# Weighing a gathered tile in four half-size operations instead of two

## The chip, the cores and the metric

The kernel runs on one core of a Trainium2 chip. The metric is device time in microseconds of one execution; the runs of the kernel before gave 2804.95, 2805.5 and 2806.83 us, a median of 2805.5 us.

## The reference

The input is 32 images of 64 channels, 128 x 128 pixels. For each image, 1024 grid points are sampled bilinearly, and from each sample a query of 64 numbers and the offsets of 8 further sampling points are computed. These 8 points are sampled bilinearly too (four corners, four weights), turned into keys and values, and attended over, head by head:

```python
q_feat = bilinear_sample(feature_map, ref)           # 1024 points of the grid
off = gelu(layer_norm(q_feat @ W_o1 + b_o1)) @ W_o2 + b_o2
sampled = bilinear_sample(feature_map, ref + off * scale)   # 8 points for each query
keys, values = sampled @ W_k.T, sampled @ W_v.T
out = softmax(q . keys) @ values                      # per head, over the 8 points
```

The 1024 tokens and a class token then pass a recurrent mixing layer (a running maximum and two running sums along the tokens, with a gated output), a feed-forward layer, and a layer in which each token uses one of 32 small experts. All of it is in float32.

## The kernel before

Images are worked on in pairs; there are 16 pairs, and 18 iterations, because a pair's work is staged: iteration `it` samples pair `it`, runs the mixing layer and the feed-forward layer (part 1) on the pair sampled before, and the experts (part 2) on the one before that. It also computes the queries and the sampling points of the pair that comes next. The first iterations and the last two are written out, the others are a loop. The last two sample nothing.

Sampling goes by tiles of 128 queries. A pair has 16 tiles (`PAIR_TILES`). For each tile:

- GpSimd (POOL) issues 8 indirect DMAs, one for each head (line 471). Each brings, for 128 queries on 128 partitions, the four corners of one head's sampling point: 4 x 64 numbers on each partition. The tile lands in one of four slots of `gathered` (`RING`). Before a tile's gathers, GpSimd waits until the tile that held the slot has been weighed: `weighted.at(it, n - RING + 1)`.
- VectorE (DVE) weighs it (`weigh`, line 1063): every corner times its bilinear weight, read from `tables` in PSUM and broadcast over the 64 channels. Two operations of 128 x 1024, one for the even heads and one for the odd ones (`e`). The result goes to one of two buffers `weighed`, laid out so that a head pair `j` (of four) and a corner `q` give 128 neighbouring columns. `weigh` waits for the slot's gathers, for the table of weights, and for TensorE to be done with the tile before the last (`points_full`).
- TensorE (PE) waits for `weighted`, and sums and transposes the tile (`sample`, line 527): 16 transposes, four corners accumulated in PSUM for each of the four head pairs. ScalarE (ACT) copies the result out (`copy_points`, line 721).
- For every two tiles TensorE projects to keys and values (`project`, line 539), VectorE scores them (`score`, lines 1075 to 1083), ScalarE takes the exponentials, and VectorE forms the attended values (`attend`, lines 1091 to 1105).

Each engine runs one instruction stream in order. An iteration has 32 slots; a tile is started every two slots, and the other work is put into slots by tables (`SCHEDULE`, `VECTOR_AT`, `SCALAR_AT`, with their own versions for the last two iterations). In VectorE's stream a slot's weighing comes first, then the scoring or attending of an earlier tile pair, then what the tables put there: the corners of the grid samples (line 988), the query features (lines 995 to 1032), the additions and products of the mixing layer on pieces of 256 columns (lines 1125 to 1185), residual additions and normalisations on 512 columns (lines 1114, 1115, 1195, 1200, 1213 to 1216, 1222), and the choice of experts (lines 1242 to 1246). Those on pieces and on 512 columns mostly have both inputs in SBUF; lines 1063, 1075, 1091, 1129, 1195, 1213, 1228 and 1253 have one input in PSUM.

In TensorE's stream a slot begins with `sample`, then comes `project` in every fourth slot, then the matmuls of parts 1 and 2 and of the query features. A wait at `sample` therefore holds all that stands behind it.

Of the kernel before, what the change touches and what calls it, by code (L numbers as in the profile page):

```python
# [7 lines left out]
ALU = mybir.AluOpType  # L8
# [6 lines left out]
P = 128  # L15
C = 64
# [4 lines left out]
HEADS = 8  # L21
# [3 lines left out]
PAIR_TILES = 2 * TILES  # L25
# [131 lines left out]
def vit_kernel(nc, pixels, grid, cls, weights, vectors, consts, shape_vectors, out):  # L157
# [40 lines left out]
    with ExitStack() as ctx:  # L198
# [3 lines left out]
        def signal(name, per=1):  # L202
            return Signal(ctx.enter_context(nc.semaphore(name)), per)
# [85 lines left out]
        slot_gathered = [signal(f"slot_gathered{k}", PAIR_TILES // RING * HEADS * 16) for k in range(RING)]  # L289
        tiles_started = signal("tiles_started", PAIR_TILES)  # L290
        weighted = signal("weighted", PAIR_TILES)
        points_full = signal("points_full", PAIR_TILES)
        points_copied = signal("points_copied", PAIR_TILES)
        kv_full = signal("kv_full", PAIR_TILES)
# [53 lines left out]
        def corners_of(s):  # L348

            return gathered[:, s, :].rearrange("p (j e q c) -> p j e q c", e=2, q=4, c=C)  # L350

        def weighed_of(n):

            return weighed[:, n % 2, :].rearrange("p (j q e c) -> p j q e c", q=4, e=2, c=C)
# [125 lines left out]
        def _(pe):  # L480
# [38 lines left out]

            def sample(it, n):  # L520

                pe.wait_ge(weighted.sem, weighted.at(it, n + 1))
                pe.wait_ge(points_copied.sem, points_copied.at(it, n))
                for j in range(HEADS // 2):
                    for q in range(4):
                        at = (4 * j + q) * 2 * C
                        mm = pe.matmul(points_ps[:, j * P:(j + 1) * P],  # L527
                                       weighed[:, n % 2, at:at + 2 * C], ident, is_transpose=True,
                                       start=(q == 0), stop=(q == 3))
                mm.then_inc(points_full.sem, 1)  # L530
# [103 lines left out]
            def iteration(it):  # L634
                for j in range(SLOTS):
                    if samples_in(it) and j % 2 == 0:
                        sample(it, j // 2)
                    if samples_in(it) and j % 4 == 3:
                        project(it, j // 4)
                    for part, names in stages(it, j):  # L640
                        if part == 1:
                            part1(it, names)
                        elif part == 2:
                            part2(it, names)
                        else:
                            prepare(it, part, names[0])
# [272 lines left out]
        def _(dve):  # L919
# [134 lines left out]
            def weigh(it, n):  # L1054

                b, t, s = n // TILES, n % TILES, n % RING
                dve.wait_ge(slot_gathered[s].sem, slot_gathered[s].at(it, (n // RING + 1) * HEADS * 16))
                dve.wait_ge(mix_ready.sem, mix_ready.at(it, b + 1))
                dve.wait_ge(points_full.sem, points_full.at(it, n - 1))
                g, to = corners_of(s), weighed_of(n)  # L1060
                wt = mix[:, t, :, :].rearrange("p (j e) q -> p j e q", e=2)
                for e in range(2):
                    ins = dve.tensor_tensor(to[:, :, :, e, :], g[:, :, e, :, :],  # L1063
                                            wt[:, :, e, :].unsqueeze(3).broadcast_to([P, HEADS // 2, 4, C]), ALU.mult)
                ins.then_inc(weighted.sem, 1)

            kv = kv_ps[:, :, :].rearrange("p a (k n) -> p (a k) n", k=4)

# [186 lines left out]
            def iteration(it):  # L1255
# [3 lines left out]
                for j in range(SLOTS):  # L1259
                    if samples_in(it) and j % 2 == 0:  # L1260
                        weigh(it, j // 2)
# [186 lines left out]
```

## Time and profile before

| | |
|---|---|
| median of 3 runs | 2805.5 us |
| the profiled execution | 2803.6 us |
| its span, first to last instruction | 2801.7 us |
| mean granted TensorE clock | 0.952 |
| busy: PE | 2391.6 us, 85% |
| busy: DVE | 2385.7 us, 85% |
| busy: POOL | 1983.2 us, 71% |
| busy: ACT | 1350.2 us, 48% |
| the 16 DMA engines, mean share in a slice of 1/40 of the span | 0 to 4 tenths |

The profile is of one execution. Busy time is the union of an engine's instructions; an instruction that only issues or waits is not counted. A group of instructions is given as line, engine, operation, written tile <- read tiles, the shape and the count, then its busy time, the mean ns of one, and the idle time of the engine just before them with what ended it. In rows of the timeline, the first number is the start in us from the span's start, the second the us that the merged instructions take from the first's start to the last's end, and the brackets give idle time before and what ended it.

### The profile page before, as it was taken

What the parts mean: (1) busy time and instruction counts of PE and PEld (TensorE: products, weight loads), DVE (VectorE), ACT (ScalarE), POOL (GpSimd) and SP (SyncE); (2) the same over time, 40 slices, a digit from 0 to 9 for tenths busy, and PEclk for the clock granted to TensorE, in tenths of its full rate; (3) what the DMA queues carried; (4) which work ended last, traced back from release to release, by engine and by line L of the source; (5) the groups of instructions that cost most, each with busy time, mean ns of one, the idle gap of its engine ahead of it and who ended that gap; (6) DMA issues with size and microseconds to landing.
All of it is one profiled execution on the core that took longest, in us unless ns stands there. A gap on an engine that the chain in (4) does not pass through costs nothing. (4 is left out here: it accounts for less than half of the span.)

```text
span 2801.7 us, 34581 instructions
## 1 busy us (share of the span) xinstructions
PE 2391.6 (85%) x10646; PEld 1561.1 (56%) x10680; DVE 2385.7 (85%) x3808; ACT 1350.2 (48%) x2326; POOL 1983.2 (71%) x2052
## 2 busy tenths in 40 slices
PE   4588889888988888898888889888888988889887
PEld 4455555655655555655555556555556556555533
DVE  5889989889998989998898989888998988888741
ACT  2345444544544444464444446444444645444563
POOL 4777777777777777777777777777777777777400
PEclk7799999999999999999999999999999999999999
DMA  4333333434343343434334343433434343333200
GB/s 161 118 119 117 119 119 103 126 118 127 118 126 118 105 123 116 127 117 127 118 111 128 108 126 118 125 118 113 127 106 126 118 125 119 111 104 103 72 0 15
DMA packets 139228, 314.70 MB, mean 112 GB/s; under 512 B 68912, under 2 KB 69296, under 8 KB 134960
## 3 DMA queue, kind: packets, MB, share of 16 engines
q0 software_dynamic: 98304, 268.57, 32.7%
q1 hardware_dynamic: 40880, 45.58, 4.8%
q8 instruction: 23, 0.38, 0.1%
q14 instruction: 21, 0.17, 0.0%
HBM read 305.62 MB, written 8.40 MB: 112 GB/s over the span
## 5 line engine op out<-in xcount | busy, mean ns | idle before, releaser
L471 POOL DMA_INDIRECT gathered<-pixels,index x2048 | 1983.0, 968 | 649.2 <-issue 614.8
L527 PE MATMUL points_ps<-c_sb,weighed 128*128 128x128 f32 x4096 | 542.4, 290 | 230.8 <-DVE weighed L1063 230.3
L1063 DVE TENSOR_TENSOR weighed<-gathered,tables 128x1024 f32<-128x1024 f32 x512 | 600.4, 1214 | 125.8 <-DMA gathered<-pixels,index 123.9
L527 PEld LDWEIGHTS points_ps<-c_sb,weighed 128*128 128x128 f32 x4096 | 494.9, 150 | 339.7 <-DVE weighed L1063 286.4
L539 PE MATMUL kv_ps<-kv_sb,sampled_t 128*128 128x256 f32 x2048 | 473.4, 385 | 26.6 <-DVE products L1091 26.4
L721 ACT ACTIVATE sampled_t<-points_ps 128x512 f32<-128x512 f32 x256 | 153.1, 598 | 710.1 <-PE points_ps L527 710.1
L539 PEld LDWEIGHTS kv_ps<-kv_sb,sampled_t 128*128 128x128 f32 x2048 | 388.0, 192 | 112.6 <-DVE products L1091 41.2
L617 PE MATMUL work_ps<-nm,w_sb 128*128 128x512 f32 x544 | 291.6, 619 | 38.0 <-DVE xm L1253 35.3
L486 PE MATMUL work_ps<-hn,w_sb 128*128 128x512 f32 x544 | 267.4, 616 | 12.9 <-DVE hn L1115 10.2
L849 ACT ACTIVATE moe_hidden<-work_ps,v_sb 128x512 f32<-128x512 f32 x272 | 186.7, 687 | 161.5 <-PE work_ps L618 144.2
L1098 DVE TENSOR_REDUCE scores<-products 128x128 f32<-128x1024 f32 x128 | 246.0, 1922 | 0.0
L624 PE MATMUL work_ps<-moe_hidden,w_sb 128*128 128x512 f32 x544 | 239.7, 593 | 0.0
L1091 DVE TENSOR_TENSOR products<-kv_ps,probs 128x1024 f32<-128x1024 f32 x128 | 155.9, 1218 | 38.3 <-ACT probs L726 31.0
L624 PEld LDWEIGHTS work_ps<-moe_hidden,w_sb 128*128 128x128 f32 x544 | 103.8, 191 | 131.0 <-issue 131.0
L617 PEld LDWEIGHTS work_ps<-nm,w_sb 128*128 128x128 f32 x544 | 93.0, 195 | 126.3 <-ACT moe_hidden L849 51.2
L486 PEld LDWEIGHTS work_ps<-hn,w_sb 128*128 128x128 f32 x544 | 93.5, 194 | 121.6 <-issue 43.2
L1078 DVE TENSOR_REDUCE scores<-products 128x128 f32<-128x1024 f32 x128 | 156.2, 1220 | 4.4
L1075 DVE TENSOR_TENSOR products<-kv_ps,queries 128x1024 f32<-128x1024 f32 x128 | 155.6, 1215 | 2.4 <-PE kv_ps L539 2.0
L587 PE MATMUL work_ps<-wide,w_sb 128*128 128x512 f32 x272 | 132.1, 632 | 27.1 <-DVE rs L1213 27.1
L786 ACT ACTIVATE wide<-work_ps,fold 128x512 f32<-128x512 f32 x136 | 91.1, 684 | 74.4 <-PE work_ps L486 74.4
L587 PEld LDWEIGHTS work_ps<-wide,w_sb 128*128 128x128 f32 x272 | 52.1, 201 | 84.8 <-issue 77.5
L618 PE MATMUL work_ps<-others_t,sel_sb 128*128 128x512 bf16 x238 | 92.9, 390 | 0.0
(169 smaller groups left out, 3124.4 us busy)
## 6 DMA issues: line engine op xcount, KB each, us to landing
grid_px<-grid SPq DMA_DIRECT2D x32, 1024.0 KB, 5.6
gathered<-pixels,index POOLq DMA_INDIRECT x2048, 2.7
out<-rm SPq DMA_DIRECT2D x32, 256.0 KB
w_sb<-weights SPq DMA_DIRECT2D x1, 1984.0 KB, 8.9
moe_hidden<-consts SPq DMA_DIRECT2D x1, 512.0 KB, 9.8
attended<-cls SPq DMA_DIRECT2D x1, 512.0 KB, 11.5
c_sb<-consts SPq DMA_DIRECT2D x1, 192.0 KB, 5.2
w_sb<-weights SPq DMA_DIRECT2D x1, 192.0 KB, 5.1
```

Source lines behind the costliest of these rows:

```text
L471: pool.indirect_dma_start(gathered[:, n % RING, k * PATCH:(k + 1) * PATCH], None, pixels, bass.IndirectOffsetOnAxis(ap=index[:, n // TILES ...
L486: pe.matmul(bank, lhsT, rhs, start=True, stop=True).then_inc(filled_now, 1)
L527: mm = pe.matmul(points_ps[:, j * P:(j + 1) * P], weighed[:, n % 2, at:at + 2 * C], ident, is_transpose=True, start=(q == 0), stop=(q == 3))
L539: mm = pe.matmul(kv_ps[:, 2 * (n % 2) + j // 2, (j % 2) * 2 * P:(j % 2 + 1) * 2 * P], sampled_t[:, n % 2, j, :], kv_sb[:, :], start=True, ...
L587: mm = pe.matmul(bank, w(W_DN + k), hidden[:, 4 * h + k, :], start=(k == 0), stop=(k == 3))
L617: pe.matmul(bank, w(W_MU + k), nm[:, cols(h)], start=True, stop=False)
L624: mm = pe.matmul(bank, w(W_MD + k), moe_hidden[:, k, :], start=False, stop=(k == 2 * BLOCKS - 1))
L849: act.activation(moe_hidden[:, k, :], bank, ACT.Relu, bias=v_sb[:, at:at + 1]).then_inc(done, 1)
L1063: ins = dve.tensor_tensor(to[:, :, :, e, :], g[:, :, e, :, :], wt[:, :, e, :].unsqueeze(3).broadcast_to([P, HEADS // 2, 4, C]), ALU.mult)
L1078: step(dve.tensor_reduce(scores[:, :, :, :].rearrange("p t k h -> p (t k h)"), products[:, :, :, :].rearrange("p t k (h d) -> p (t k h) d" ...
L1091: dve.tensor_tensor(products[:, :, :, :].rearrange("p t k (h d) -> p (t k) h d", h=HEADS), kv[:, :, C:2 * C].rearrange("p k (h d) -> p k h ...
L1098: mark(dve.tensor_reduce(scores[:, :, :, :].rearrange("p t k h -> p t (k h)"), products[:, :, :, :].rearrange("p t k c -> p t c k"), AX_X, ...
```

## The change

The weighing becomes four operations of 128 x 512: first the even and odd heads of head pairs 0 and 1, then those of pairs 2 and 3. A new semaphore `half_weighted` is raised after the second of them, `weighted` after the fourth. TensorE waits for `half_weighted` before the transposes of head pairs 0 and 1, and for `weighted` before those of pairs 2 and 3. Nothing else is changed; GpSimd still waits for `weighted`.

```diff
@@ def sample(it, n) (TensorE)
-                pe.wait_ge(weighted.sem, weighted.at(it, n + 1))
+                pe.wait_ge(half_weighted.sem, half_weighted.at(it, n + 1))
                 pe.wait_ge(points_copied.sem, points_copied.at(it, n))
                 for j in range(HEADS // 2):
+                    if j == HEADS // 4:
+                        pe.wait_ge(weighted.sem, weighted.at(it, n + 1))
                     for q in range(4):
@@ def weigh(it, n) (VectorE)
-                for e in range(2):
-                    ins = dve.tensor_tensor(to[:, :, :, e, :], g[:, :, e, :, :],
-                                            wt[:, :, e, :].unsqueeze(3).broadcast_to([P, HEADS // 2, 4, C]), ALU.mult)
-                ins.then_inc(weighted.sem, 1)
+                for j, done in ((slice(0, HEADS // 4), half_weighted), (slice(HEADS // 4, HEADS // 2), weighted)):
+                    for e in range(2):
+                        ins = dve.tensor_tensor(to[:, j, :, e, :], g[:, j, e, :, :],
+                                                wt[:, j, e, :].unsqueeze(3).broadcast_to([P, HEADS // 4, 4, C]), ALU.mult)
+                    ins.then_inc(done.sem, 1)
```

## Rows read from the trace of the kernel before

**Rows 1.** The page's costliest groups: gathers, transposes, weighing; busy, mean ns | idle before.

```profile
L471 POOL DMA_INDIRECT gathered<-pixels,index x2048 | 1983.0, 968 | 649.2 <-issue 614.8
L527 PE MATMUL points_ps<-c_sb,weighed 128*128 128x128 f32 x4096 | 542.4, 290 | 230.8 <-DVE weighed L1063 230.3
L1063 DVE TENSOR_TENSOR weighed<-gathered,tables 128x1024 f32<-128x1024 f32 x512 | 600.4, 1214 | 125.8 <-DMA gathered<-pixels,index 123.9
```

**Rows 2.** The gathers' own line: ns of one, least/median/most, first and last start.

```profile
L471 POOL DMA_INDIRECT gathered<-pixels,index x2048: 942/946/1468, 26.1 to 2631.7; - x187
```

**Rows 3.** Waits: engine, line, waited for: us in total, times, longest us.

```profile
POOL gathered L471 <- DVE weighed L1063: 8.8, 29, 0.3
...
DVE weighed L1063 <- DMA gathered<-pixels,index: 123.9, 68, 4.5
```

**Rows 4.** Busy time by stretch, one iteration's length in the loop: us, busy (x).

```profile
1363.00:1526.00 163.00, 142.27 (x662) 95.16 (x663) 147.52 (x233) 81.65 (x142) 124.01 (x129) 0.98 0.40 119
```

**Rows 5.** Timeline, 1331 to 1344 us, VectorE and GpSimd.

```profile
1331.10 2.35 DVE L1063 TENSOR_TENSOR weighed<-gathered,tables 128x1024 f32<-128x1024 f32 x2 [0.62 <-DMA gathered<-pixels,index]
...
1335.38 0.69 DVE L1216 TENSOR_TENSOR hm<-h,x 128x512 f32<-128x512 f32 x1
1335.81 1.07 POOL L471 DMA_INDIRECT gathered<-pixels,index  x1 [0.30 <-issue]
...
1343.17 0.69 DVE L1216 TENSOR_TENSOR hm<-h,x 128x512 f32<-128x512 f32 x1
1343.45 1.22 POOL L471 DMA_INDIRECT gathered<-pixels,index  x1 [0.30 <-issue]
```

**Rows 6.** Timeline, 1361 to 1367 us, VectorE and GpSimd.

```profile
1362.81 2.35 DVE L1063 TENSOR_TENSOR weighed<-gathered,tables 128x1024 f32<-128x1024 f32 x2
1364.02 0.94 POOL L471 DMA_INDIRECT gathered<-pixels,index  x1 [0.30 <-issue]
1365.07 0.69 DVE L1114 TENSOR_TENSOR x<-xc,rs 128x512 f32<-128x512 f32 x1
1365.27 1.31 POOL L471 DMA_INDIRECT gathered<-pixels,index  x1 [0.30 <-DVE weighed L1063]
1365.68 0.69 DVE L1115 TENSOR_TENSOR hn<-xc,rs 128x512 f32<-128x512 f32 x1
```

**Rows 7.** Timeline, 1398 to 1411 us, VectorE and GpSimd.

```profile
1398.06 0.86 DVE L1125 SCALAR_TENSOR_TENSOR hn<-xc,decay,state_o 128x256 f32<-128x256 f32 x2
1398.22 1.12 POOL L471 DMA_INDIRECT gathered<-pixels,index  x1 [0.31 <-issue]
...
1409.44 1.42 DVE L1141 TENSOR_TENSOR xc<-wide,rs 128x256 f32<-128x256 f32 x4
1409.64 1.03 POOL L471 DMA_INDIRECT gathered<-pixels,index  x1 [0.30 <-issue]
```

**Rows 8.** Timeline, 1416 to 1438 us, VectorE and GpSimd.

```profile
1419.67 1.42 DVE L1157 TENSOR_TENSOR hn<-wide,state_q 128x256 f32<-128x256 f32 x4
1420.19 1.05 POOL L471 DMA_INDIRECT gathered<-pixels,index  x1 [0.31 <-issue]
...
1436.97 1.42 DVE L1185 TENSOR_TENSOR wide<-wide,hn 128x256 f32<-128x256 f32 x4
...
1437.16 1.04 POOL L471 DMA_INDIRECT gathered<-pixels,index  x1 [0.30 <-DVE weighed L1063]
```

**Rows 9.** Timeline, 1433 to 1444 us: a tile's transposes, and VectorE behind them.

```profile
1437.10 3.45 PE L527 MATMUL points_ps<-c_sb,weighed 128*128 128x128 f32 x16 [4.40 <-DVE weighed L1063]
...
1441.45 0.69 DVE L1195 TENSOR_TENSOR x<-x,work_ps 128x512 f32<-128x512 f32 x1 [3.06 <-PE work_ps L486]
...
1442.31 0.69 DVE L1195 TENSOR_TENSOR x<-x,work_ps 128x512 f32<-128x512 f32 x1 [0.17 <-PE work_ps L486]
...
1442.91 1.22 DVE L1075 TENSOR_TENSOR products<-kv_ps,queries 128x1024 f32<-128x1024 f32 x1
```

**Rows 10.** Timeline, 2600 to 2680 us: the last tile pair's projection and what it waits for.

```profile
2640.06 3.72 PE L539 MATMUL kv_ps<-kv_sb,sampled_t 128*128 128x256 f32 x16 [1.22 <-DVE products L1091]
```

More of the change, by code:

```diff
@@ L291, in vit_kernel @@
         weighted = signal("weighted", PAIR_TILES)
+        half_weighted = signal("half_weighted", PAIR_TILES)
         points_full = signal("points_full", PAIR_TILES)
```

## The prediction

> **What bounds the kernel now.** The page's groups come first. PE and DVE are each 85% busy, so one looks for the end among them, but the first group is the gathers: 2048 of 968 ns, and before them 649.2 us of idle time, of which 614.8 end with nothing but the issue itself [rows 1]: 0.30 us before every gather in the timeline [rows 5 to 8]. The gathers' own line gives the median, 946 ns, and the first and last start, 26.1 and 2631.7 us [rows 2]. From start to start that is (2631.7 - 26.1) / 2047 = 1.273 us, the 0.968 and the 0.30: GpSimd runs one chain without a hole, 93% of the span. The waits confirm it: GpSimd's waits for weighing are never longer than 0.3 us, which is the issue time, while weighing waits 68 times for a gather, 123.9 us in all [rows 3]. In an iteration's 163 us DVE has work for 147.5 and PE for 142.3 [rows 4]. They lag in places and catch up; neither stops the chain. What ends the kernel is therefore the chain of gathers and a tail of 170 us behind it.
>
> One thing can lengthen this chain. The mean gather is 22 ns above the median, 2048 x 22 ns = 45 us in all [rows 1, 2], and the timeline shows where from. A gather that starts while DVE runs an operation with both inputs in SBUF lasts longer, by what is left of that operation less 0.13 us. L1114 runs from 1365.07 to 1365.76; the gather that starts at 1365.27 lasts 1.31, so 0.36 too long, and 1365.76 - 1365.27 - 0.13 = 0.36 [rows 6]. L1216 leaves 0.26 and 0.41 at two gathers, which last 0.12 and 0.27 too long [rows 5]. Inside a weighing, which reads its weights from PSUM, the gather at 1364.02 has its 0.94 us [rows 6]. So these stalls are a matter of phase between DVE's stream and the gathers, and what moves DVE's stream moves the time.
>
> The Trainium skill has the rule: "SBUF — State Buffer", section "SBUF: two separate sides", says that a DVE operation with two SBUF inputs and a GpSimd instruction lock a shared port pair, whoever starts first, for the whole instruction. The trace agrees for the gather behind the operation. It doesn't for the other order: L1115 starts at 1365.68 inside that gather and takes its usual 0.69 us [rows 6]. By the page DVE would wait there too, and each growth below would be given back where the next such operation starts in the held gather.
>
> **The change, part by part.** *DVE.* Two operations of 1024 columns become four of 512. What counts is the distance from one start to the next. Two weighing operations take 1365.07 - 1362.81 = 2.26 us [rows 6]. An operation of 512 columns takes 1365.68 - 1365.07 = 0.61 with both inputs in SBUF [rows 6] and 1442.91 - 1442.31 = 0.60 with one in PSUM [rows 9], and weighing is of that kind. Four take 2.40 us: 0.14 us more for a tile. From below this can't be under 0, as no work is dropped; from above it is 0.32 if the recorded lengths did not overlap (4 x 0.69 [rows 9] less 2 x 1.214 [rows 1], rounded). I take 0.14, since both its terms are read directly. An iteration gets 16 x 0.14 = 2.2 us more on DVE, 149.7 of 163 us: still no bound.
>
> The Trainium skill, "Perfetto Trace Analysis", section on optimizing Scalar/DVE operations, gives some 125 ns for each DVE access to PSUM; by that the two added operations would cost 0.25 us a tile, and the sum below would be 21 us instead of 12.
>
> *PE.* The first half is done after 1.20 us instead of 2.26, and its eight transposes run beside the second half. Where PE waits for weighing, what is left after the last weighing is eight transposes instead of 16, so a tile is ready earlier by eight of them (542.4 / 4096 x 8 = 1.06 us [rows 1], 1.7 where 16 take 3.45 [rows 9]) less DVE's 0.14. PE waited 230.3 us for weighing before these transposes [rows 1]; with 256 tiles that is 0.9 us a tile, and up to all of it may go. But nothing on the path receives them: ACT's copy and the projection come earlier, and DVE, which gets to the scores in its own order, is late next. Where DVE itself waits for PE (3.06 us before L1195 [rows 9]) it arrives earlier, which shifts its phase and no more. The two half waits hold nothing longer than the one did: the second ends 0.14 us later than `weighted` did, with eight transposes behind it instead of 16.
>
> *GpSimd.* It waits for `weighted`, 0.14 us later. Its waits now show the issue time alone [rows 3], so the cost is 0; the cover is the ring of four tiles, and gone only if DVE lagged a tile or more further.
>
> *The stalls.* Here the 0.14 us go. A gather that was stalled starts again when DVE's operation ends, so from then on both run in step, and a later stall is what it was, until another weighing puts 0.14 us into DVE's stream. At the next stall, DVE's operation ends 0.14 us later against the gather, and the gather is held 0.14 us longer, as long as it still starts within the operation. Where a weighing follows a wait for gathers, DVE is in step with GpSimd again, and the count starts anew; a weighing directly before such a wait adds nothing. One iteration, 1331 to 1492 us, gone through tile by tile:
> - Stalls that grow by 0.14: behind tile 0 (L1216 at 1335.38; the gather starts 0.43 us after it [rows 5]); behind tile 3 (L1114, 0.20 [rows 6]); behind tiles 7, 8 and 9 (L1141, L1157's second piece, L1185, each 0.19 to 0.20 [rows 7, 8]); behind tiles 4 and 5 two of the same kind. Seven, 0.98 us.
> - The second L1216 at 1343.17 has no weighing between it and the first: unchanged [rows 5].
> - Tiles 1 and 15 come before a wait for gathers: nothing.
> - Open: behind tile 6 the gather starts 0.16 us into L1125 and is stalled 0.17 us [rows 7]; a shift of 0.14 leaves 0.02 us, and a little more puts the gather in front, and the stall is gone: +0.14 or -0.17. Tile 2 (an operation released by ACT), 13 and 14 likewise. Tiles 10 to 12 come behind the wait at L1195 that PE's head start moves [rows 9]. Net taken as 0, at most +0.14 for each of seven, about +1.0 us.
>
> Three quarters of 0.98, since in other iterations some gathers will start just ahead of the operation and not in it: 0.75 us an iteration, x 16 = 12 us. The ends: seven stalls that all go (0.12 + 0.36 + 0.08 + 0.10 + 0.09 from the five shown [rows 5 to 8], some 0.09 for the two others, 0.84 an iteration) give -13 us; all grown, 16 x 1.98 = +32 us.
>
> *The tail.* The last projection waits for DVE's L1091 and not for its points [rows 10], and DVE comes to it 0.14 us later: +0.1 us, and -0.9 if the points had been last. Neither can be told.
>
> Sum: 2803.6 + 12 = 2815.6 us for the profiled execution, whose own time is 1.9 us under the median of the runs; at the median 2817.5 us.
>
> **The rivals.** All times at the median. A measurement of this kernel can tell about 0.2%, 5.6 us, from no change.
> - *Hidden after all.* The chain of gathers is untouched, DVE's 0.14 us are lost in its waits (DVE idles 15 us of 163 [rows 4]), and stalls that go balance those that grow. For it: the open places above have both signs. Against it: the waits that absorb are four or so an iteration [rows 3], and at most of the stalls the gather starts deeper in the operation than 0.14 us. 2800 to 2811, middle 2805.5 us.
> - *Faster.* PE's head start takes DVE's waits for PE from it, its stream runs ahead by up to 1 us, and the stalls are dealt anew and come out smaller; it decides from the point where the shift exceeds the depth of the gather in the operation (0.16 to 0.43 us [rows 5 to 8]). Its price is at most the -13 us above; half gives 2799 us. Against it: nothing favours small stalls. The Trainium skill ("Perfetto Trace Analysis", the same section) says that breaking up DVE instructions may finish work sooner when DVE is not saturated but causes bubbles on other engines. The bubbles are there [rows 1], but on an engine that isn't the bound.
> - *A costlier half operation*, the 0.32 of the upper end: 16 x 0.32 = 5.1 us an iteration, DVE at 152.6 of 163, still no bound; but the stalls would grow by 0.32 each, 27 us or 2832 us, unless they pass the operations' starts.
> - *The change does not do what it says*: PE comes too late to the first half to use it. Then PE gains nothing, and the time is that of the forecast.
>
> **How the numbers follow.** Forecast, stalls grow: 0.68; its own range is 2809 to 2829 us, and 0.03 of it lie within 0.2% (under 2811). Hidden: 0.21, all of it within. Faster: 0.07, of which 0.02 within. The costlier operation: 0.04. That gives faster 0.05, within 0.2% 0.26, slower 0.69. The change doing less than it says has no chance of its own, since its time is the forecast's. The whole range starts at 2803, well into the hidden case, and ends at 2829, short of all stalls grown.
>
> **What would show it.** Four weighing operations of some 0.68 us, 2.40 us from the first start to the next operation's. PE's idle time before the transposes down by a third or more. GpSimd's waits for weighing still at 0.3 us. Median gather still 946 ns, mean up by 12 us / 2048 = 6 ns, to 974; last gather's start near 2644 us. Stalls at L1216, L1114, L1141, L1157 and L1185 longer by 0.14. The prediction is wrong if the mean gather stays at 968 or falls, if GpSimd waits for weighing, or if the time comes with an unchanged last gather.

## The result, and the profile after

The changed kernel takes 2819.82 us (median of 5 runs, 2816.27 to 2824.82) against 2805.5 us before (2804.3 to 2806.83): ratio 1.0051, 95% interval [1.0039, 1.0063], 14 us slower. The profiled execution is the slowest of the five, 2824.82 us with a span of 2823.0, and one single gather explains 6.8 us of that (below).

The page's groups, and its line for the queue that brings instructions (packets, MB, share), of the kernel after:

```profile
q14 instruction: 82, 0.67, 0.1%
...
L472 POOL DMA_INDIRECT gathered<-pixels,index x2048 | 2002.6, 978 | 649.5 <-issue 618.4
L1067 DVE TENSOR_TENSOR weighed<-gathered,tables 128x512 f32<-128x512 f32 x1024 | 633.7, 681 | 156.7 <-DMA gathered<-pixels,index 124.1
...
L530 PE MATMUL points_ps<-c_sb,weighed 128*128 128x128 f32 x4096 | 551.1, 290 | 170.4 <-DVE weighed L1067 165.5
```

Beside [rows 1]: 2048 gathers are busy 19.6 us longer (1983.0 before), and the time between them is what it was (649.2 before). PE's wait for weighing fell from 230.3 to 165.5 us, so PE did get its head start, and the kernel became slower all the same. The gathers' own line, as [rows 2]:

```profile
L472 POOL DMA_INDIRECT gathered<-pixels,index x2048: 942/946/7759, 26.4 to 2651.7; - x187
```

The median is still 946 ns, and the last gather starts 20.0 us later. The most is new: one gather of 7.76 us. Take its 6.8 us away, and the last start is 2644.9. The waits, as [rows 3], with one kind that was not there before:

```profile
DVE weighed L1067 <- DMA gathered<-pixels,index: 124.1, 58, 4.4
DVE x L1199 <- PE work_ps L487: 40.6, 33, 2.9
DVE weighed L1067 <- issue: 32.0, 12, 2.8
...
POOL gathered L472 <- DVE weighed L1067: 5.2, 17, 0.3
```

GpSimd never waits longer than its issue time for weighing. VectorE waits 12 times for nothing that the trace shows, 2.7 us each. One iteration's length, as [rows 4]:

```profile
1363.00:1526.00 163.00, 145.03 (x655) 95.94 (x654) 147.92 (x263) 80.31 (x139) 124.01 (x129) 0.95 0.40 119
```

Neither PE (142.27 before) nor DVE (147.52) came to its bound. Where the gathers' time went is seen in the timeline of VectorE and GpSimd, at the places of [rows 5 to 8]. GpSimd's line moved by 1, PE's by 3, VectorE's by 4: L1216 is now L1220, L1114 L1118, L1141 L1145, L1157 L1161, L1185 L1189.

```profile
1347.81 0.69 DVE L1220 TENSOR_TENSOR hm<-h,x 128x512 f32<-128x512 f32 x1
1348.14 1.17 POOL L472 DMA_INDIRECT gathered<-pixels,index  x1 [0.30 <-issue]
...
1355.59 0.69 DVE L1220 TENSOR_TENSOR hm<-h,x 128x512 f32<-128x512 f32 x1
1355.88 1.22 POOL L472 DMA_INDIRECT gathered<-pixels,index  x1 [0.30 <-issue]
...
1374.89 2.48 DVE L1067 TENSOR_TENSOR weighed<-gathered,tables 128x512 f32<-128x512 f32 x4
1377.28 0.69 DVE L1118 TENSOR_TENSOR x<-xc,rs 128x512 f32<-128x512 f32 x1
1377.39 1.40 POOL L472 DMA_INDIRECT gathered<-pixels,index  x1 [0.30 <-DVE weighed L1067]
...
1422.03 1.42 DVE L1145 TENSOR_TENSOR xc<-wide,rs 128x256 f32<-128x256 f32 x4
1422.10 1.17 POOL L472 DMA_INDIRECT gathered<-pixels,index  x1 [0.30 <-issue]
...
1432.39 1.42 DVE L1161 TENSOR_TENSOR hn<-wide,state_q 128x256 f32<-128x256 f32 x4
1432.79 1.17 POOL L472 DMA_INDIRECT gathered<-pixels,index  x1 [0.30 <-issue]
...
1449.84 1.43 DVE L1189 TENSOR_TENSOR wide<-wide,hn 128x256 f32<-128x256 f32 x4
1449.91 1.17 POOL L472 DMA_INDIRECT gathered<-pixels,index  x1 [0.30 <-issue]
```

Read the depth first, how far into VectorE's operation the gather starts, then its length. At L1145 the depth is 0.07 (1422.10 - 1422.03) where it was 0.20 [rows 7], and the gather lasts 1.17 where it lasted 1.03. L1189 went from 0.19 and 1.04 [rows 8] to 0.07 and 1.17, L1161 from 1.05 to 1.17. The first L1220 went from 1.07 to 1.17; the second, with no weighing between, kept its 1.22 [rows 5]. At these places VectorE came later by 0.10 to 0.13 us, and each gather was held by that much longer.

Summed over the execution, by the VectorE operation that runs when a gather starts (us over the median gather, times; worked out from all 2048 gathers; a selection of lines by their numbers before, and all of them together):

```
                              before     after
L1141 (piece of 256)          1.2, 14    3.3, 16
L1157                         1.3, 13    3.0, 14   without the one of 7.76 us
L1185                         2.0, 16    3.0, 13
L1216 (512 columns)           5.4, 28    7.8, 30
L1114                         6.5, 18    3.3, 8
L1115                         1.2, 3     4.7, 11
L1243 (choice of experts)     1.2, 15    2.9, 15
all gathers                   45.6       58.4      without the one of 7.76 us
```

The stalls grew by 12.8 us. What follows the last gather took 170.3 us (169.1 before), and the first started 0.4 us later. These three make 14.4 us, and that is the whole loss of the profiled execution without the one long gather: 2824.8 - 6.8 = 2818.0 us against 2803.6 before.

### The profile page after: what moved, and what is told of

Same layout as the page of the kernel before. It is cut to its first block and busy times, and to the rows that moved or that the text cites. A ratio compares the mean times of both kernels' runs of the same rounds, so it can differ in the third digit from the quotient of the medians.

```text
span 2823.0 us, 35127 instructions
## 1 busy us (share of the span) xinstructions
PE 2430.4 (86%) x10680; PEld 1569.4 (56%) x10680; DVE 2418.1 (86%) x4320; ACT 1351.2 (48%) x2326; POOL 2002.8 (71%) x2052
## 5 line engine op out<-in xcount | busy, mean ns | idle before, releaser
L1067 DVE TENSOR_TENSOR weighed<-gathered,tables 128x512 f32<-128x512 f32 x1024 | 633.7, 681 | 156.7 <-DMA gathered<-pixels,index 124.1
L530 PE MATMUL points_ps<-c_sb,weighed 128*128 128x128 f32 x4096 | 551.1, 290 | 170.4 <-DVE weighed L1067 165.5
L620 PE MATMUL work_ps<-nm,w_sb 128*128 128x512 f32 x544 | 298.1, 631 | 44.7 <-DVE xm L1257 43.5
L590 PE MATMUL work_ps<-wide,w_sb 128*128 128x512 f32 x272 | 141.9, 672 | 48.1 <-DVE rs L1217 48.1
L621 PE MATMUL work_ps<-others_t,sel_sb 128*128 128x512 bf16 x272 | 107.8, 396 | 0.0
```

What stands on the lines that cost most here:

```text
L530: mm = pe.matmul(points_ps[:, j * P:(j + 1) * P], weighed[:, n % 2, at:at + 2 * C], ident, is_transpose=True, start=(q == 0), stop=(q == 3))
L590: mm = pe.matmul(bank, w(W_DN + k), hidden[:, 4 * h + k, :], start=(k == 0), stop=(k == 3))
L620: pe.matmul(bank, w(W_MU + k), nm[:, cols(h)], start=True, stop=False)
L1067: ins = dve.tensor_tensor(to[:, j, :, e, :], g[:, j, e, :, :], wt[:, j, e, :].unsqueeze(3).broadcast_to([P, HEADS // 4, 4, C]), ALU.mult)
```

## The experiments

Theories: *stalls* (what VectorE's stream does 0.13 us later holds gathers longer), *head start* (PE's earlier transposes do the harm), *fetch* (the 12 unexplained waits of VectorE do it). Ratios are to the kernel before on the same chip, in the same set of runs: 2804.85 us for the whole wait, the delay and the two kernels with ones; 2808.56 for the two moved loops, the shorter delay and the six operations in pieces; 2806.01 for the last four (wider, longer loop, more delay, three operations in pieces).

**PE waits for the whole tile, four weighings kept.**

```diff
-                pe.wait_ge(half_weighted.sem, half_weighted.at(it, n + 1))
+                pe.wait_ge(weighted.sem, weighted.at(it, n + 1))
...
-                    if j == HEADS // 4:
-                        pe.wait_ge(weighted.sem, weighted.at(it, n + 1))
```

> Four half weighings as in the changed kernel, but TensorE waits for the whole tile before its first transpose, so its head start is gone. Stall theory (0.14 us more of VectorE's time for each tile moves its two-SBUF-input operations against the gathers): the slowdown stays, +8 to +18 us on the kernel before, mean gather 972 to 980 ns. Head-start theory (TensorE being earlier changes when VectorE runs and deals the stalls anew): back to within 5 us of the kernel before, mean gather near 968 ns.

Measured: 2823.99 us, ratio 1.0064 [1.0052, 1.0077]. Its waits:

```profile
PE points_ps L528 <- DVE weighed L1065: 252.9, 87, 11.3
```

PE waits as long as before the change, longer even, and the slowdown is whole. The head start does no harm, and no good beyond the intervals.

**A delay behind two whole weighings**, by writing 160 spare columns of PSUM.

```diff
                 ins.then_inc(weighted.sem, 1)
+                dve.wait_ge(delayed.sem, delayed.at(it, n))
+                dve.memset(tables[:, T_SPARE:T_SPARE + 160], 0.0).then_inc(delayed.sem, 1)
```

> The kernel before, with its two whole weighings, and behind each tile's weighing a memset of 160 spare PSUM columns, which should take some 0.14 us of VectorE and reads nothing in SBUF. No half weighing, no head start for TensorE. Stall theory: +8 to +18 us, mean gather 972 to 980 ns, and the longer stalls where the changed kernel has them. If it is the half weighing itself or the head start that costs the time: within 5 us of the kernel before.

Measured: 2808.96 us, ratio 1.002 [1.0011, 1.0029]; slower than before, but less than expected. The delay turned out larger than the change's: from the first weighing's start to the end of the scoring product behind it (median of 50 tiles) it is 3.68 us, 3.48 before and 3.61 after, so 0.20 us against 0.13. This kernel, too, has 12 waits of VectorE at the head of a turn (32.5 us in all). The timeline of this kernel, VectorE and GpSimd:

```profile
1411.23 0.94 POOL L473 DMA_INDIRECT gathered<-pixels,index  x1 [0.30 <-issue]
1411.24 1.45 DVE L1145 TENSOR_TENSOR xc<-wide,rs 128x256 f32<-128x256 f32 x4
1412.48 1.03 POOL L473 DMA_INDIRECT gathered<-pixels,index  x1 [0.30 <-issue]
```

The gather that was held at a depth of 0.20 [rows 7] now starts 0.01 us ahead of the operation and passes in 0.94; the next meets the fourth piece at its own 0.20 and lasts 1.03. The delay used up the depth, and the stall is back to what it was. That suggests a test that no theory but *stalls* passes: more delay on top of the change should make it faster (below).

**No operation left to hold a gather.** In the kernel before and in the changed one, the operations on 256 and 512 columns of the mixing layer, the feed-forward layer and the residual additions get a column of ones in PSUM as second operand, in place of the one that the reference asks for.

```diff
-                mark(dve.tensor_tensor(x1[:, cols(h)], xc[:, cols(h)], rs1[:, cols(h)], ALU.mult))
+                mark(dve.tensor_tensor(x1[:, cols(h)], xc[:, cols(h)], one_ps.broadcast_to([P, HALF]), ALU.mult))
...
```

> The kernel before, in which VectorE's operations on 256 and 512 columns of the mixing layer, the feed-forward layer and the residual additions read a column of ones in PSUM in place of their second SBUF operand (their values are therefore not the reference's; lengths and order stay). Stall theory: the gathers lose nearly all of their 45 us of stalls, mean gather 947 to 950 ns, time 2762 to 2770 us. If the long gathers had another cause that only coincides: mean gather near 968 ns, time near 2805 us.

> The changed kernel with the same PSUM operands as the one before it in this set (its values are not the reference's). Stall theory: as that one within 3 us, some 2762 to 2771 us, so the half weighings cost nothing where there is nothing to stall on. If the added time came from VectorE's own lateness (its longer stream, or its twelve waits of 2.7 us at the loop's turn): 8 us or more above that one.

Measured: 2763.83 us for the kernel before, ratio 0.9849 [0.9836, 0.9862], and 2765.48 us for the changed one, 0.9856 [0.9842, 0.9871]. The gathers' group on the page, before with ones, then after with ones:

```profile
L472 POOL DMA_INDIRECT gathered<-pixels,index x2048 | 1943.0, 949 | 649.6 <-issue 615.2
```

```profile
q14 instruction: 82, 0.67, 0.1%
...
L473 POOL DMA_INDIRECT gathered<-pixels,index x2048 | 1943.5, 949 | 648.8 <-issue 616.8
```

The mean gather is within 3 ns of the median in both, and 41 us are gone (2804.85 - 2763.83): the stalls that the prediction read out of [rows 1, 2] are real, 45 us of them, and an operand in PSUM ends them. With nothing to be held by, the change costs 1.65 us instead of 14, though VectorE still waits 12 times at the head of a turn (82 instruction packets). That speaks for *stalls* and against *fetch*, and bounds what *fetch* can cost where nothing is held.

**Moving VectorE's loop among its instructions**, before and after: 240 and 260 satisfied waits ahead of the iterations.

```diff
+            for _ in range(240):
+                dve.wait_ge(constants_set.sem, 1)
             all_iterations(dve, iteration, vector_steps)
```

> The kernel before, with 240 waits that are already satisfied put ahead of VectorE's iterations, so that its loop stands at another place among its instructions; the iterations are as before. Stall theory (the change costs time because later VectorE operations hold gathers for longer): VectorE may wait some 2.7 us once in each of 12 turns of the loop, as in the changed kernel, but it catches up, the gathers' mean stays at 967 to 971 ns and the time is within -2 to +6 us of before. Fetch theory (the changed kernel lost its time to these waits at the loop's turn): 10 to 15 us slower.

> The changed kernel, with 260 satisfied waits ahead of VectorE's iterations. Both theories: VectorE's waits of 2.8 us in each turn vanish, and the instruction queue is back near 21 packets. Stall theory: the slowdown stays, 8 to 16 us over before, with the gathers' mean at 972 to 979 ns. Fetch theory: at most 3 us over before, gathers' mean 970 ns or less.

Measured: 1.0007 [0.9998, 1.0016] and 1.0049 [1.0037, 1.0062]. The times are as *stalls* had it, but the premise was wrong: the shifted kernel before has no such waits, and the shifted changed one keeps them, so the pair says nothing on *fetch*. (Two of these waits go into one instruction; the shift was 120 and 130.) What does order them is the length of the loop's body: VectorE's records in the trace from one turn to the next are 314 to 322 in the six kernels of this study that have none, and 326 to 363 in the eight that have them.

**A shorter delay**: 16 spare columns instead of 160, and 280 waits ahead of the iterations.

```diff
+                dve.wait_ge(delayed.sem, delayed.at(it, n))
+                dve.memset(tables[:, T_SPARE:T_SPARE + 16], 0.0).then_inc(delayed.sem, 1)
```

> The kernel before, with a small VectorE operation (16 spare columns in PSUM) and a satisfied wait behind each tile's two weighings, which put off what follows them by some 0.12 to 0.14 us a tile, as the change does; the weighings stay whole, PE starts when it did, and 280 satisfied waits ahead of the iterations keep the loop free of waits at its turn. Stall theory: the later VectorE operations start later against the gathers, the stalls at the operations behind the weighings grow (L1141, L1157, L1185 of before by 0.1 us each and more), the mean gather takes 972 to 978 ns, and the time is 8 to 16 us over before. Rivals (the half weighings themselves hold gathers, or PE's early start does the harm): within 4 us of before.

Measured: 2817.4 us, ratio 1.0031 [1.002, 1.0043]. The delay was 0.06 us (3.54 against 3.48), not 0.12, and the stalls at L1141 and L1185 of before grew by that: median gathers there 1.09 and 1.10 us, where before has 1.02 and 1.04 and after 1.17 and 1.17. Whole weighings and no head start, and still half the delay gives 0.6 of the loss (0.0031 of 0.0051). Two things weaken this run. The 280 waits did not keep the loop free: its turn has 331 records, and VectorE waits 12 times, 32.7 us in all. And in its profiled execution the stalls, without one gather of 8.44 us, sum to 50.5 us, 4.9 more than before, where the time grew by 8.8.

**The same delay without an added instruction**: the second weighing of a tile covers 128 columns more, eight in each of 16 rows. The rows of `weighed` are longer by these eight, and the two heads of a pair change places in the gathered tile.

```diff
+                    width = C + (EXTRA if e == 0 else 0)
...
-                    ins = dve.tensor_tensor(to[:, :, :, e, :], g[:, :, e, :, :],
+                    ins = dve.tensor_tensor(to[:, :, :, (1 - e) * C:(1 - e) * C + width], source,
```

> The kernel before, with the second weighing of each tile made 128 columns wider (eight more columns in each of its 16 rows, written to columns that nobody reads), which puts off what follows by 0.13 us a tile and adds no instruction: the loop stays at 314, the weighings at two, and PE starts after the whole tile. Stall theory: the dose is that of the change, so the stalls grow as there, the gathers' mean is 973 to 979 ns, the time 8 to 16 us over before, with no waits at the loop's turn. Rival (the loss needs those waits, or the half weighings): within 4 us of before.

Measured: 2825.05 us, ratio 1.006 [1.0042, 1.0079]. The page, and then VectorE and GpSimd in its timeline at L1185 of before, here L1190:

```profile
q14 instruction: 21, 0.17, 0.0%
...
L473 POOL DMA_INDIRECT gathered<-pixels,index x2048 | 2004.6, 979 | 649.4 <-issue 621.8
```

```profile
1452.34 1.42 DVE L1190 TENSOR_TENSOR wide<-wide,hn 128x256 f32<-128x256 f32 x4
1452.40 1.17 POOL L473 DMA_INDIRECT gathered<-pixels,index  x1 [0.30 <-issue]
```

No waits at the turn (21 packets, as before), two weighings a tile, no head start: 0.13 us of delay, the same depth, the same 1.17, and a loss as large as the change's. So the loss needs neither the waits nor half weighings nor the head start, and this run decides between the theories. Not all of its loss is stalls, though. Over its own median they are 54.2 us without one gather of 7.76 us, 8.6 more than before; its median gather is 949 ns instead of 946, which is 6 us over 2048, and what sets that stays open. Its ratio is above that of the changed kernel, within the intervals.

**A longer loop with the same work**: 16 satisfied waits ahead of L1195, where VectorE waits for PE.

```diff
             def add_mix(it):
+                if not isinstance(it, int):
+                    for _ in range(16):
+                        dve.wait_ge(constants_set.sem, 1)
```

> The kernel before, with 16 waits that are already satisfied inside VectorE's loop, ahead of the sums of L1195, where VectorE waits some 3 us for PE anyway: the loop grows from 314 to 330 instructions and its work keeps its times. Both theories: VectorE waits 2.7 us at the head of 12 turns, as every kernel so far with a longer loop. Stall theory: VectorE catches up within some tiles, the gathers' mean stays at 967 to 972 ns, and the time is within 3 us of before. Fetch theory (the changed kernel lost its time to these waits): 6 to 14 us over before.

Measured: ratio 1.0003 [0.9987, 1.0019], but with no waits at the turn: the 16 became 8 instructions, 322 records in a turn instead of 330, and that is under the length at which they begin. It tells nothing on *fetch* beyond that length.

**More delay on top of the change.**

```diff
                     ins.then_inc(done.sem, 1)
+                dve.wait_ge(delayed.sem, delayed.at(it, n))
+                dve.memset(tables[:, T_SPARE:T_SPARE + 16], 0.0).then_inc(delayed.sem, 1)
```

> The changed kernel, with a small VectorE operation and a satisfied wait behind each tile's four weighings, some 0.06 us a tile, so that the later operations are put off by 0.19 us in all, as in the run with the longer delay. Stall theory: the delay passes the depth at which several operations no longer run when a gather starts (L1141, L1157, L1185 of before), so the time falls although VectorE does more: 3 to 9 us over before, 4 us or more under the changed kernel, gathers' mean 967 to 973 ns. Rival (each nanosecond of VectorE's time adds to the loss): 14 to 22 us over before.

Measured: 2810.42 us, ratio 1.0008 [0.9992, 1.0024], apart from the changed kernel's [1.0039, 1.0063]. VectorE does more, and the kernel is faster. Its profiled execution was the slowest of 12 (2828.22 us, the others 2808.53 to 2821.48), with twice the waits at the turn, one long gather and a mean gather of 979 ns, where 967 to 973 was expected; no trace shows the stalls of a run near the median. Two lines show what they should all the same: the gathers at L1141 and L1185 of before have medians of 1.03 and 0.98 us. At L1141 the edge itself is seen: eight gathers that start 0.017 to 0.029 us into the operation pass in 0.95 us, and five that start 0.032 to 0.035 us into it are held to 1.20 or 1.21.

The delays side by side (us a tile, by the distance to the scoring product), a hump and not a slope:

```
0.00  no change of VectorE's work       1.0003 and 1.0007
0.06  short delay                       1.0031
0.13  change, whole wait, moved, wider  1.0051, 1.0064, 1.0049, 1.0060
0.19  change and short delay            1.0008
0.20  long delay                        1.0020
```

Of these kernels the wider one and the two of the first row have no waits at the turn, the others have them.

**Shorter operations to be held by.** All six products and sums on 512 columns that read two tiles in SBUF in pieces of 256, and then only three of them (L1115, L1200, L1216).

```diff
-                dve.tensor_tensor(hm[:, cols(h)], h0[:, cols(h)], x1[:, cols(h)], ALU.add).then_inc(hm_ready.sem, 1)
+                for k in range(2):
+                    last = dve.tensor_tensor(hm[:, part_of(h, k)], h0[:, part_of(h, k)], x1[:, part_of(h, k)], ALU.add)
+                last.then_inc(hm_ready.sem, 1)
```

> The kernel before, with the six products and sums on 512 columns that read two tiles in SBUF (L1114, L1115, L1200, L1215, L1216, L1222 of before) done in pieces of 256 columns, and 300 satisfied waits ahead of the iterations against waits at the loop's turn. Stall theory: a gather that starts beside one of them is held for the rest of a shorter operation, so the stalls at these lines fall from some 20 us to some 10 us, and the time by 3 to 12 us. Rival: the added VectorE time moves other operations into the gathers' starts, and the time is within 3 us of before.

> The kernel before, with only the products L1115 and L1200 and the sum L1216, 512 columns each, done in two pieces of 256 (the loop grows to 320 instructions). Stall theory: their stalls, 10 us in all before, fall to 6 us or less, and the time by 2 to 6 us. Rival: the pieces add 0.06 us each to VectorE and the operations behind them meet other gathers, so that it is within 2 us of before.

Measured: all six 2806.15 us, ratio 0.9993 [0.9984, 1.0002], no difference; three 2801.22 us, ratio 0.9975 [0.9963, 0.9988], faster than both kernels. The gathers of the two on their pages:

```profile
L474 POOL DMA_INDIRECT gathered<-pixels,index x2048 | 1984.3, 969 | 651.5 <-issue 611.9
```

```profile
L474 POOL DMA_INDIRECT gathered<-pixels,index x2048 | 1980.0, 967 | 650.0 <-issue 614.2
```

With three cut, the stalls at their lines fall from 9.9 us to 5.2 (L1216 5.4 to 2.9, L1115 and L1200 4.5 to 2.3), and all stalls from 45.6 to 42.6. With six, the stalls over the median fall further, to 40.7, but the median itself is 949 ns, 6 us more over 2048, the first gather starts 1.5 us later and the end comes 2.5 us later behind the last. Its loop is long enough for the waits at the turn (326 records), that of three is not (320).

## Why the prediction was right, point by point

- *What bounds the kernel.* Right. With the stalls gone the kernel is 41 us faster without a faster PE or VectorE, and GpSimd's waits for weighing stay at 0.3 us.
- *Four operations cost 0.14 us a tile.* Nearly: 0.13 us (3.61 - 3.48), 681 ns for one. (The upper bound of 0.32 is 0.33 by its own terms; no run came near it.) The Trainium skill, "Perfetto Trace Analysis", section on optimizing Scalar/DVE operations, by which the two more would have cost an estimated 0.25 us, is not borne out here: 0.065 us each.
- *PE's head start is real and off the path.* Right in kind: the time is the same with it and without, within the intervals. Its size was overstated: the idle time before the transposes fell by 28%, not by a third or more.
- *GpSimd does not wait.* Right: 17 waits, at most 0.3 us.
- *The stalls grow by the delay.* Right in mechanism and sum: 12 us forecast, 12.8 found; the mean gather 974 ns forecast, 978 found, of which the one long gather makes 3.3; the last start 2644 forecast, 2644.9 without it. Four of the five lines grew: the gathers at L1141, L1157 and L1185 went from 1.03, 1.05 and 1.04 us to 1.17 each, the one at the first L1216 gained 0.10, the one at the second nothing, as said.
- *L1114* was the miss among them. It grew from 1.31 to 1.40 where it still holds a gather, but does so 8 times instead of 18; 11 gathers instead of 3 now meet L1115 behind it. Together they stay (7.7 us before, 8.0 after). One of the 11, in the timeline of VectorE and GpSimd:

```profile
1536.82 1.28 DVE L1226 TENSOR_TENSOR nm<-xm,rm 128x512 f32<-128x512 f32 x2
1537.05 1.28 POOL L472 DMA_INDIRECT gathered<-pixels,index  x1 [0.31 <-issue]
...
1539.89 0.95 POOL L472 DMA_INDIRECT gathered<-pixels,index  x1 [0.31 <-issue]
1540.42 0.69 DVE L1118 TENSOR_TENSOR x<-xc,rs 128x512 f32<-128x512 f32 x1
1541.02 0.69 DVE L1119 TENSOR_TENSOR hn<-xc,rs 128x512 f32<-128x512 f32 x1
1541.14 1.39 POOL L472 DMA_INDIRECT gathered<-pixels,index  x1 [0.30 <-issue]
```

  These are not the gathers just ahead of an operation for which the prediction had set a quarter of the growth aside: one starts 0.53 us ahead of L1114 (here L1118), and the next 0.12 us into L1115. They go with PE's head start: 11, 10 and 10 gathers are held at L1115 in the three kernels that have it (changed, moved, more delay), three in each of the two with the same 0.13 us and no head start (whole wait, wider). So the head start does deal some stalls anew, at no gain.
- *The sum was near in part by luck.* The five lines, with L1115, grew by 7.5 us of the 12.8, where 0.14 us, 16 times, by three quarters gives 8.4 for five. The prediction had 3.4 more for two places behind tiles 4 and 5 that it did not name; the rest of the growth came at places that it counted at nothing or left open, as the experts' choice (L1243, +1.7 us) and the query features (L1003 to L1008, +2.1).
- *Faster, by passing the depth.* Not at 0.13 us, but the rival's point of decision is real: at 0.19 to 0.20 us more than half of the loss is gone again.
- *Not foreseen:* the waits at the loop's turn, 32 us of VectorE's time that cost the kernel little (the whole change costs 1.65 us where nothing is held, with 12 such waits in it); and the one long gather.

## What to carry to other kernels

Where one engine issues a chain without a hole, look for what lengthens its single links: a mean above the median is the sign, and the timeline shows which engine's operation it ends with. Then an edit on an engine that is not the bound is priced by where it moves that engine's operations against the chain, and the price need not grow with the delay: try a few delays before judging an edit. Better still, take away what does the holding: give long operations beside the chain an operand in PSUM, or make the worst of them shorter, and only those.

## What the runs showed of the hardware

**Waits at the loop's turn.** VectorE in the changed kernel, at the head of a turn:

```profile
537.57 0.69 DVE L1220 TENSOR_TENSOR hm<-h,x 128x512 f32<-128x512 f32 x1
540.99 2.48 DVE L1067 TENSOR_TENSOR weighed<-gathered,tables 128x512 f32<-128x512 f32 x4 [2.73 <-issue]
```

They come with some 61 more packets on the instruction queue (81 to 83 against 21 or 22), in every kernel with 326 or more VectorE records in a turn, in none with up to 322, wherever the loop was moved to. The kernel with more delay waits 24 times and not 12, with no more packets (82). The Trainium skill, "Runtime: NRT & Kernel Launch", section "Instruction fetch mechanics", says that a taken branch to instructions no longer held forces a fetch before the engine goes on. The packets agree with it, but do not tell why that kernel waits twice as often; that it sets in between 322 and 326 records, and costs 2.7 us a turn in the changed kernel, is from these runs alone.

**One long gather.** GpSimd in the changed kernel:

```profile
280.87 1.00 POOL L472 DMA_INDIRECT gathered<-pixels,index  x1 [0.31 <-issue]
282.17 7.76 POOL L472 DMA_INDIRECT gathered<-pixels,index  x1 [0.30 <-issue]
290.23 0.95 POOL L472 DMA_INDIRECT gathered<-pixels,index  x1 [0.30 <-issue]
```

Seven of the 14 profiled executions have exactly one gather of 7.8 or 8.4 us, at times from 117 to 2578 us, in kernels of either kind; the other seven have none over 2.1 us. No operation of VectorE lasts that long. What it is stays open, and so does how often it comes in executions without a profile. The five kernels that lose 0.3% or more all have one in their profiled execution, of the other nine two. Part of their median loss could be such gathers; for the changed kernel the sum above does without it. The two kernels with ones in PSUM have none, and their nine executions lie within 1.8 us for each kernel.

**The hold goes one way.** VectorE's operations that start inside a gather keep their length: L1161's four pieces take 1.42 us beside a gather of 1.17, as in [rows 8]. In the kernel before, the 115 operations of L1114, L1115, L1200, L1216 and L1222 that start inside a gather have a median of 684 ns, the 55 others 685. The lock in both directions that the Trainium skill states ("SBUF — State Buffer", section "SBUF: two separate sides") for VectorE operations with two inputs in SBUF and GpSimd instructions that read SBUF is not seen in that direction here.
